# Own-key corners of a causal maximum moved from matmul masks to a copy, a GpSimd mask and one reduction

## What is computed

```
mod = (silu(c) @ wmod).reshape(1, 6, 1, -1)          # sa, ca, ga, sb, cb, gb
scores = einsum('bqhd,bkhd->bhqk', q_full, k_full) * softmax_scale
scores = where(causal, scores, finfo.min)
attn = softmax(scores, axis=-1);  out = attn @ v
x = x + ga * attention(layernorm(x) * (1 + ca) + sa)
x = x + gb * ffn(layernorm(x) * (1 + cb) + sb)
```

## Time and profile before

| | us |
|---|---|
| runs (3): median, lowest, highest | 820.46, 819.85, 820.5 |
| the profiled execution, whole | 820.3 |
| its span from first to last instruction | 818.2 |
| granted TensorE clock over the span | 0.985 |

### The profile page before, as it was taken

One profiled execution on the slowest core, in us unless ns is written; L12 is line 12 of the kernel. 1 busy time (PEld: TensorE's weight loads), 2 busy tenths in 40 slices (PEclk: granted clock), 3 DMA queues, 4 the chain that ended last, 5 costly groups with the idle time before them and its releaser, 6 DMA issues.

```text
span 818.2 us, 10342 instructions
## 1 busy us (share of the span) xinstructions
PE 768.3 (94%) x3901; PEld 497.2 (61%) x3901; DVE 551.6 (67%) x847; ACT 275.0 (34%) x394; POOL 152.2 (19%) x132
## 2 busy tenths in 40 slices
PE   3898899999999999999999998999897999999997
PEld 2755455555555555555555555454786788886886
DVE  6877679789789789789789788677565222223342
ACT  4722233333333333333333332334243322222110
POOL 1136314024014014014024010010243000000111
PEclk9999899999999999999999998999998999999999
DMA  8333603303303303403403470253000142210011
GB/s 310 148 81 78 151 15 78 93 2 78 93 0 78 93 1 78 93 1 78 93 1 78 107 306 0 74 191 123 1 1 0 41 115 77 78 30 0 26 39 39
DMA packets 36144, 60.72 MB, mean 74 GB/s; under 512 B 4256, under 2 KB 16288, under 8 KB 34304
## 3 DMA queue, kind: packets, MB, share of 16 engines
q1 hardware_dynamic: 36096, 60.06, 26.2%
HBM read 32.66 MB, written 2.10 MB: 42 GB/s over the span
## 4 chain that ended last, share of the span: by engine, by line
PE 62%; DVE 22%; issue 9%; POOL 3%; ACT 2%; DMA 1%; POOLq 0%; SPq 0%; DVEq 0%; ACTq 0%
PE PS L747 15%; DVE PR L1243 6%; PE PS L653 6%; PE PS L590 6%; PE PS L668 6%; PE PS L717 6%; PE PS L654 5%; PE PS L655 5%; DVE NMa L1146 4%; DVE NMb L1146 3%; PE PS L580 3%; PE PS L606 2%; PE PS L657 2%; PE PS L594 1%; POOL OT L1527 1%
## 5 line engine op out<-in xcount | busy, mean ns | idle before, releaser
L884 ACT ACTIVATE PR<-PS 128x1024 f32<-128x1024 f32 (+1 forms) x144 | 132.9, 929 | 262.2 <-PE PS L655 247.2
L1146 DVE TENSOR_REDUCE NMa<-PS 128x1 f32<-128x512 f32 (+3 forms) x216 | 138.6, 662 | 46.0 <-PE PS L594 40.7
L590 PE MATMUL PS<-KH,Q 96*128 96x512 f32 (+3 forms) x384 | 132.3, 404 | 5.8 <-DVE NMa L1146 2.8
L653 PE MATMUL PS<-Q,KH 97*128 97x512 f32 x288 | 131.7, 457 | 0.0
L747 PE MATMUL PS<-Q 128*128 128x512 f32 (+1 forms) x528 | 122.9, 395 | 5.1 <-DVE Q L1342 4.5
L1243 DVE TENSOR_TENSOR PR<-PR 128x2048 f32<-128x2048 f32 (+3 forms) x56 | 109.3, 1951 | 10.8 <-ACT PR L884 9.7
L747 PEld LDWEIGHTS PS<-Q 128*128 128x128 f32 (+1 forms) x528 | 99.2, 188 | 28.2 <-DVE Q L1342 4.7
L654 PE MATMUL PS<-Q,KL 96*128 96x512 f32 x288 | 115.0, 399 | 0.0
L655 PE MATMUL PS<-Q,KH 96*128 96x512 f32 x288 | 114.2, 397 | 0.0
L590 PEld LDWEIGHTS PS<-KH,Q 96*128 96x128 f32 x384 | 68.0, 192 | 61.7 <-issue 35.8
L653 PEld LDWEIGHTS PS<-Q,KH 97*128 97x128 f32 x288 | 56.2, 195 | 31.8 <-issue 13.7
(11 more groups left out here) (177 smaller groups left out, 955.6 us busy)
## 6 DMA issues: line engine op xcount, KB each, us to landing
Q<-TQ SPq DMA_DIRECT2D x64, 384.0 KB, 6.0
RT<-in_wo SPq DMA_DIRECT2D x4, 1024.0 KB, 4.7
TQ<-in_wo SPq DMA_DIRECT2D x4, 1024.0 KB, 4.9
WI<-in_gate_w SPq DMA_DIRECT2D x10, 256.0 KB, 3.4
WI<-in_up_w SPq DMA_DIRECT2D x10, 256.0 KB, 3.6
DI<-in_down_w SPq DMA_DIRECT2D x10, 256.0 KB, 3.7
PR<-in_wmod_c SPq DMA_DIRECT2D x2, 1024.0 KB, 6.2
x_in<-in_x SPq DMA_DIRECT2D x8, 256.0 KB, 9.9
```

The source lines that it names most:

```text
L590: ins = pe.matmul(bank[:, i * w:(i + 1) * w], M.Q[0:KR, g % 2, 0, qt // 4, h0 + i, qs], M.KH[0:KR, lo:lo + w], start=(i == 0), stop=(i == ...
L653: pe.matmul(dst, M.KH[0:KR + 1, ks], M.Q[0:KR + 1, w % 2, 0, qb, :, qs], start=True, stop=False)
L884: act.activation(tiles, banks, ACT.Exp).then_inc(S_.p, 1)
L1146: dve.tensor_reduce(dst, PS[:, bank_of(turn), 0:n * w].rearrange("p (h k) -> p h k", k=w), axis=AX.X, op=ALU.max, negate=True).then_inc(S_ ...
```

## The change

The mask products of the maxima go. ACT copies the 128 own-key columns of the 22 parts from PSUM into an SBUF tile of four heads (`diag`, two of them), GpSimd masks the tile with one `affine_select`, and DVE reduces it in one instruction (`least`), two query tiles later. A part of qt 1 to 3 and 5 to 7 that ends on own keys is reduced by DVE without its last 128 columns, after ACT's copy; the two parts of only own keys (qt 0 and the second of qt 4) are not reduced by DVE, and ACT frees their bank. The parts stand by query tile, own-key part first. `join` takes one minimum more. HANDED goes: DVE makes group 1's products too. The rotated queries lie in RT instead of a buffer of their own, so `even` waits for the end of the previous split. The late modulation columns become eight items of one instruction in window 7, their loads stand behind x, wv and wo, and `load_chunk(0)` waits for them; wv and the gate's scratch get places of their own.

```diff
@@ maxima_parts @@
-    return sorted(parts, key=lambda part: (part[0] >= NS // 2, part[3] + part[4]))
+    return sorted(parts, key=lambda part: (part[0], -part[1], part[3]))
-HANDED = (1,)
+def is_diagonal(k):
+    qt, lo, w, _, _ = PARTS[k]
+    return lo + w == (qt + 1) * P
+def is_shared(k):
+    return is_diagonal(k) and PARTS[k][2] > P
@@ maxima_places @@
-    cost = [0.14 + w * n / 960 for _, _, w, _, n in PARTS]
+def reduce_cost(k):
+    _, _, w, _, n = PARTS[k]
+    left = w - P if is_diagonal(k) else w
+    return 0.14 + left * n / 960 if left else 0.0
+    cost = [max(reduce_cost(k), 0.3) for k in range(len(PARTS))]
+        if qt >= 2 and k == LAST_PART[qt - 1] + 1:
+            places.append((place, ("least", qt - 2), 0.65))
+        places.append((place, ("part", k), reduce_cost(k)))
+        if k in LAST_PART:
+            places.append((place, ("diag", qt), 0.0))
+    return places + [(end, ("least", NS - 2), 0.65), (end + 0.01, ("least", NS - 1), 0.65)] + [(end + 0.02, ("join",), 0.1), (end + 0.07, ("rows",), 0.3)]
@@ window_table @@
+        places += group_places(w, [(0.38 + 0.06 * (KD * n + d), ("mod", 2 + n, d), 0.6) for n in range(2) for d in range(KD)])
-    if w == G - 2:
-        places += [(0.45 + 0.2 * n, ("mod", w, 2 + n), 2.5) for n in range(2)]
@@ sp_program @@
-            load_columns(2)
-            load_columns(3)
...
             load_wo(1)
+            load_columns(2)
+            load_columns(3)
...
+    sp.wait_ge(S_.mc, 2 + 2 * KD)
     load_chunk(0)
@@ pe_program, maxima_part @@
-        if diagonal:
-            corner = bank[:, 0:n * w].rearrange("p (h k) -> p h k", k=w)[:, :, w - P:]
-            ins = pe.matmul(corner, M.identb[:], M.maskb[:].unsqueeze(1).broadcast_to([P, n, P]), start=False, stop=True)
@@ act_program @@
+    def diagonal_copied(g, k):
+        qt, lo, w, h0, n = PARTS[k]
+        turn = TURN[("part", g, k)]
+        done = NS * g + qt - 1
+        act.wait_ge(S_.side, turn + 1)
+        if done > 0:
+            act.wait_ge(S_.dm, done)
+        corner = PS[:, bank_of(turn), 0:n * w].rearrange("p (h k) -> p h k", k=w)[:, :, w - P:]
+        act.activation(M.diag[:, qt % 2, h0:h0 + n, :], corner, ACT.Copy).then_inc(
+            S_.dc if is_shared(k) else S_.free[turn % 3], 1)
@@ dve_program @@
     def even(g, hf):
-            dve.wait_ge(S_.re, 2 * half)
+            dve.wait_ge(S_.tl, half)
     def part_reduced(g, k):
+        left = w
+        if is_shared(k):
+            dve.wait_ge(S_.dc, len(SHARED) * g + SHARED.index(k) + 1)
+            left = w - P
+    def diagonal_reduced(g, qt):
+        dve.wait_ge(S_.ds, NS * g + qt + 1)
+        dve.tensor_reduce(M.NMd[:, qt // 4, :, qt % 4], M.diag[:, qt % 2], axis=AX.X, op=ALU.max,
+                          negate=True).then_inc(S_.dm, 1)
     def join(g):
-        dve.tensor_tensor(M.NMa[:, 1], M.NMa[:, 1], M.NMb[:], ALU.min).then_inc(S_.nm, 1)
+        dve.tensor_tensor(M.NMa[:, 1], M.NMa[:, 1], M.NMb[:], ALU.min).then_inc(S_.nj, 1)
+        dve.wait_ge(S_.nj, g + 1)
+        dve.wait_ge(S_.dm, NS * (g + 1))
+        dve.tensor_tensor(M.NMj[:], M.NMa[:], M.NMd[:], ALU.min).then_inc(S_.nm, 1)
@@ pool_program @@
+    def diagonal(g, qt):
+        tile = M.diag[:, qt % 2]
+        for k in range(len(PARTS)):
+            if PARTS[k][0] == qt and is_diagonal(k) and not is_shared(k):
+                pool.wait_ge(S_.free[TURN[("part", g, k)] % 3], freed(("part", g, k)))
+        shared = [i for i, k in enumerate(SHARED) if PARTS[k][0] == qt]
+        if shared:
+            pool.wait_ge(S_.dc, len(SHARED) * g + shared[-1] + 1)
+        pool.affine_select(out=tile, in_=tile, compare_op=ALU.is_ge, fill=MASKED, base=0, pattern=[[0, HG], [-1, P]],
+                           channel_multiplier=1).then_inc(S_.ds, 1)
```

More of the change, by code:

```diff
@@ L197, in __init__ @@
         self.RT = take("RT", [P, 4, 512])
-        self.RE = take("RE", [P, 2, 512])
+        self.diag = take("diag", [P, 2, HG, P])
+        loaded = self.at
         self.WP = take("WP", [P, 2 * P])
@@ L314 @@
 SLACK = 0.04
+def reduce_cost(k):
+    _, _, w, _, n = PARTS[k]
+    left = w - P if is_diagonal(k) else w
+    return 0.14 + left * n / 960 if left else 0.0
 def maxima_places(begin, end):
[L318 to L320 removed]
+    cost = [max(reduce_cost(k), 0.3) for k in range(len(PARTS))]
+    places = []
+    for k in range(len(PARTS)):
+        qt = PARTS[k][0]
+        place = begin + (end - begin) * sum(cost[:k]) / sum(cost)
+        if qt >= 2 and k == LAST_PART[qt - 1] + 1:
[4 more added lines that the diff above has]
+    return places + [(end, ("least", NS - 2), 0.65), (end + 0.01, ("least", NS - 1), 0.65)] + [(end + 0.02, ("join",), 0.1), (end + 0.07, ("rows",), 0.3)]
 def group_places(g, places):
[L325 to L326 removed]
+    return [(place, (name[0], g) + name[1:], busy) for place, name, busy in places]
 def window_table(w):
@@ L686, in pe_program @@
         side(key)
-    pe.wait_ge(S_.mask, 4)
+    pe.wait_ge(S_.mask, 6)
     pe.wait_ge(S_.one, 1)
@@ L832, in weights_high @@
         act.activation(M.WH[:], M.WF[:], ACT.Copy).then_inc(S_.wh, 1)
-    def queries_copied(kind, g, hf):
-        turn = TURN[(kind, g, hf)]
+    def diagonal_copied(g, k):
+        qt, lo, w, h0, n = PARTS[k]
+        turn = TURN[("part", g, k)]
+        done = NS * g + qt - 1
         act.wait_ge(S_.side, turn + 1)
[L837 to L846, removed]
-        act.activation(M.TQ[:, 2, 0, cols], PS[:, bank_of(turn), :], ACT.Copy).then_inc(S_.lh, 1)
+        if done > 0:
[3 more added lines that the diff above has]
+            S_.dc if is_shared(k) else S_.free[turn % 3], 1)
     def split_high(g, hf):
@@ L1205, in side @@
             weights_folded(g, key[2])
-        elif kind == "even" and g not in HANDED:
+        elif kind == "even":
             even(g, key[2])
-        elif kind == "odd" and g not in HANDED:
+        elif kind == "odd":
             odd(g, key[2])
@@ L1213, in side @@
             split_low_first(key[2])
-        elif kind == "part":
+        elif kind == "part" and (is_shared(key[2]) or not is_diagonal(key[2])):
             part_reduced(g, key[2])
+        elif kind == "least":
+            diagonal_reduced(g, key[2])
         elif kind == "join":
@@ L1479, in side @@
             weights_low(g)
-        elif kind == "even" and g in HANDED:
-            rotate_even(g, key[2])
-        elif kind == "odd" and g in HANDED:
-            rotate_odd(g, key[2])
+        elif kind == "diag":
+            diagonal(g, key[2])
         elif kind == "odd" and (g, key[2]) != (0, 1):
```

113 lines of the change are left out of this document (53 added, 60 removed).

## The result

The changed kernel takes 856.89 us (median of four runs, 856.5 to 859.45) against 820.48 for the kernel before on the same chip: a ratio of 1.0455, 95% interval 1.0434 to 1.0476; the medians lie 36.4 us apart. One of the four runs of the kernel before took 1462.04 us and is left out of the ratio; the other three took 819.85 to 820.5. The forecast was 830, its range ended at 846. The sign was right and so was the ring of waits; the half clock behind the ring, which the sum put at nothing, was not.

A forecast was written before the change was run, and what follows sets the result against it. Each window was taken as bound by PE (31.2 us), then DVE (25.9), then PE (3.9). Prologue +4.9, windows 0 to 5 +10.8, window 6 -6.8 and window 7 +0.7 made +9.6 on 820.3: 830 us, range 807 to 846.

The forecast's parts named there:

- the ring: Units 2 to 3 of a window: ACT's corner copies, DVE's reductions and exponentials wait for each other; PE waits 1.7 us.
- A window, summed: Windows 0 to 5: PE -0.8, ring +1.7, `den` +0.3, corner +0.35, join +0.25, giving +1.8 us each.
- The wait before the turned maxima: End of a window: PE's wait of 1.01 us for DVE's join becomes 2.4.
- Masks off PE: Mask products ahead of the hand-over to DVE in each window, removed from PE: -2.0 us.
- DVE's stretch: Window behind the hand-over, where DVE is the bound: it keeps its 24.4 us of work.
- the join: End of a window: the join's second minimum waits for the first, +0.25 us.
- the corner: DVE's stretch: tile 6's first corner goes DVE, ACT, DVE, leaving 0.35 us idle.
- the forecast's list of signs: What traces would show, among it PE waiting over 1 us in unit 3 and DVE without gaps from the denominators on.
- Windows 6 and 7: Window 6 loses late sums and masks, -6.8 us; window 7 takes the eight sums, +0.7.
- Prologue: Maxima of group 0: DVE takes back group 1's products and copies, 6.7 less 1.8 for the join: +4.9 us.
- The sum: Whole kernel: 4.9 + 10.8 - 6.8 + 0.7 = +9.6 us on 820.3, forecast 830.
- The rival with the clock: Half clock behind the wait before the turned maxima: +19 us in six windows, 849; in two, 836; chance 0.24.

The follow-up runs named there:

- held kernel: The changed kernel with idle products on PE in its waits (unit 3, before the turned maxima, the prologue's maxima), all waits kept: 848.37 us, ratio 1.0336.
- without corners: The changed kernel with all masks as products on PE and every part reduced whole, as before the change, everything else kept: 820.75 us, ratio 1.0003.
- four tiles and a busy PE: The changed kernel with four corner tiles instead of two and idle products on PE in its waits: 830.83 us, ratio 1.012.
- the kernel with the low corners: The changed kernel with the new corner route for query tiles 0 to 3 alone, tiles 4 to 7 masked on PE: 859.28 us, ratio 1.0473.
- late_only: The kernel before with only the late modulation sums spread as eight items in window 7, their loads behind x, wv and wo: 814.17 us, ratio 0.9923.

## Why the prediction was right or wrong

*The ring: right.* A wait of 1.7 us was forecast; PE is idle 1.48 us in unit 3 (4.52 with 3.04 of work), through the links named. Unit 3 as a whole grew by 2.1 us on the mean of the six windows, 2.4 in window 3.

*The step that failed: "A window, summed" carries no clock for the ring.* The forecast looked for half clock behind one wait only, that before the turned maxima, and gave it a chance of 0.24 as a rival. It took the ring's wait as 1.7 us and no more. In the trace the granted clock falls behind the ring in each of windows 0 to 5 (0.51 over units 4 and 5 of window 3, 0.67 in windows 1, 2, 4 and 5). Over the six windows the half clock costs some 10 us behind the ring and some 5 behind the turned maxima; these are estimates, the stretches up to unit 2 and from unit 4 to 16 less the same stretches of the held kernel, where the clock stays at 1.00. The ring's waits themselves are 8.7 us, and the held kernel shows that a PE kept busy in them keeps its clock. The Trainium skill (TensorE: Matmul & The Clock Gate, "A second HAM failure mode: psum-queue depth-cycling") says that PE which idles briefly between groups of products while it cycles through banks can lose its clock over and over. The trace agrees, though the page tells of another kernel, in bf16: here 3.04 us of work in 4.52, then 0.51. That page spoke against the change, and the forecast did not weigh it.

*The wait before the turned maxima: right, but the clock was low behind two of six only.* It grew from 1.01 to 2.17 us (2.4 forecast). PE's timeline, two of these waits in the changed kernel:

```profile
295.53 0.27 PE L632 MATMUL PS<-ident,NMj 128*32 128x128 f32 x1 [2.17 <-DVE NMj L1198]
...
362.65 0.37 PE L632 MATMUL PS<-ident,NMj 128*32 128x128 f32 x1 [2.17 <-DVE NMj L1198]
```

The table by stretch for the 6 us behind each (the granted clock is the third number from the right):

```profile
295.53:301.53 6.00, 6.00 (x36) 3.17 (x36) 3.86 (x4) 2.11 (x3) 0.00 (x0) 1.00 0.43 103
362.65:368.65 6.00, 6.00 (x20) 3.21 (x20) 3.17 (x3) 1.02 (x1) 0.00 (x0) 0.50 0.19 52
```

Six times the same wait, one in each of windows 0 to 5; the clock was low behind two of them (162.68 and 362.65). So the forecast's guess that the clock decides from a wait between 1.01 and 1.89 us did not hold.

*Masks off PE: over-priced.* 11 masks over one head at 0.125 us, and four larger ones, made 2.0 a window; doubling them costs 1.1, about 0.07 each. Taking a mask away gives less still. PE's timeline shows a product of 512 columns and the next product, in the kernel before with a mask between them:

```profile
292.74 0.39 PE L590 MATMUL PS<-KH,Q 96*128 96x512 f32 x1
...
293.01 0.48 PE L653 MATMUL PS<-Q,KH 97*128 97x512 f32 x1
```

In the changed kernel, without one:

```profile
319.28 0.39 PE L625 MATMUL PS<-KH,Q 96*128 96x512 f32 x1
319.51 0.39 PE L685 MATMUL PS<-Q,KH 97*128 97x512 f32 x1
```

The starts are 0.27 us apart with the mask and 0.23 without. Behind the last product of 256 columns it is 0.16 and 0.12, behind the last of four of 128 columns 0.16 and 0.11. So a mask is worth 0.04 to 0.05 us whatever its width, and the 15 of them some 0.7 us a window (an estimate from these spacings). In the changed kernel nothing of it shows: units 6 to 16 take 0.8 us more than without corners.

*DVE's stretch: nearly right.* +0.25 for the join and +0.35 for the corner were forecast; it took 0.84 more, 0.4 of it without corners too, by the new order and the second minimum. Its work stayed the same, as forecast; but DVE stands idle for 1.25 us of it (25.57 busy of 26.82), where the forecast's list of signs had it without gaps. Tile reductions at 0.673 us are as slow as those of 512 columns from PSUM (0.67), which is what was taken for them. The Trainium skill (VectorE: DVE Perf Modes, the perf-mode tier table) has it so, and the trace agrees. GpSimd's masks took 0.778 on the mean (0.7 taken), and the four long sums behind the second denominators are not slower for them: 9.7 us together against 10.3 before (why: last section).

*Windows 6 and 7: right for the late sums* (-6.8 and -0.1 where -6.5 and +0.7 were expected; the run without the other parts was forecast to 0.5 us). In the changed kernel 1.7 us of it are given back (52.2 against 50.5). The 3.0 us for window 6's masks did not come: PE is busy 49.63 us there against 50.51 in the run with the late sums alone, both at 1.00.

*Prologue: +4.9 against +8.8, and for a wrong reason.* The 6.2 us of products are worth 0.1 alone. The new order and the shared place cost 3.7 with the clock that fell, the corner route 5.1, of which 4.4 go with four tiles and a busy PE.

*The sum.* By windows +1.8 each against +5.2 on the mean: 2.1 from unit 3, 0.8 from DVE's stretch, and some 2.2 from the half clock (an estimate: the 15 us above, less some 2 that window 0 loses to it in the kernel before). PE's saving of 0.8 a window did not come. The rival with the clock was the right family, but at the wrong place: it counted on the join only. Had the ring been charged with one stretch of half clock (3.2 us, the forecast's own price from window 6), six windows would have added 19, and the sum would have been 849. That would have been nearer partly by luck, since the half clock behind the ring cost some 10.

## What to carry to other kernels

Price a new wait of TensorE with the half clock that can follow it, and every such wait, not the longest one only: the clock cost as much here as the waiting. A product on the bound engine whose removal gives 0.04 us is a poor thing to trade for three hand-overs; a route over a second engine lengthens the time that a bank is held, and with three banks that is what stops PE. And double an operation before taking it away: one run could have told that the masks were worth 6.4 us at most. It is an upper end only, for it prices a second mask (1.1 us a window), and the spacing of products with and without one says less (0.7).

## What the runs showed of the hardware

The length of a single wait did not decide whether the clock fell: behind 2.17 us it stayed at 1.00 four times of six, and in the kernel with the low corners it was low behind waits of 1.41. One of these in PE's timeline of that kernel:

```profile
291.06 0.37 PE L639 MATMUL PS<-ident,NMj 128*32 128x128 f32 x1 [1.41 <-DVE NMj L1205]
```

The table by stretch just before the wait, within it, and for the 6 us behind it:

```profile
288.80:289.80 1.00, 0.85 (x4) 0.21 (x2) 1.00 (x3) 0.00 (x0) 0.00 (x0) 1.00 0.00 0
290.00:291.00 1.00, 0.00 (x0) 0.00 (x0) 0.74 (x3) 0.00 (x0) 0.00 (x0) 0.50 0.00 0
...
291.06:297.06 6.00, 6.00 (x19) 2.89 (x20) 4.24 (x3) 1.62 (x2) 0.00 (x0) 0.52 0.19 53
```

The wait began at 289.65, and at 290.00 the clock is already at its lower level: this fall cannot be the work of the whole wait.

The first maxima product starts between 59.8 and 60.3 us in seven of the profiled executions and between 62.0 and 63.5 in the other eight. In these eight, and in no other, the clock is at its lower level in a stretch between 22 and 42 us, while PE works on the prologue. PE's first product starts at 11.9 to 12.7 us in all fifteen, so the input loads explain 0.8 us at most. What made the clock fall there stays open. There is one trace of each kernel, but the spans of one kernel differ by as much (810.7 to 814.2 us in the four runs of `late_only`).

A GpSimd mask takes 0.63 us alone and 1.88 beside a long sum of DVE (at 354.50 in the changed kernel). That sum ran from 353.05 to 355.89, and the mask ended at 356.38, 0.49 us behind it: of the two, the one that started later stood. The sum itself took 2.84 us instead of 2.28, not for this mask but for the last 0.69 us of a GpSimd operation that had started at 351.33. The same pairs stand in each of windows 0 to 5, so the masks cost the long sums nothing here: each that met one came second.
